# Maxima over hid's blocks from absolute values of the second butterfly stage, in place of one strided reduction

## The chip, the cores and the metric

One core of a Trainium2 chip runs the whole kernel. The metric is the device time of the program in microseconds, in the median of several runs. TensorE multiplies matrices into PSUM, VectorE and ScalarE work elementwise on SBUF and PSUM, GpSimd on SBUF alone, SyncE issues the transfers. The engines run their own instruction lists and wait for each other by semaphores.

## What is computed

The input x has 64 sequences of 64 tokens with 512 features. First x gets an attention layer's output added (a conditioned input, 16 heads, ALiBi); then a feed-forward layer's. The change lies in the second quantized product of that feed-forward layer:

```python
def fwht(x):                       # normalized Walsh-Hadamard transform of the last axis
    ...
def act_quant(x, bits):
    qb = float(2 ** (bits - 1) - 1)
    scale = qb / jnp.clip(jnp.max(jnp.abs(x), axis=-1, keepdims=True), EPS, None)
    q = jnp.clip(jnp.round(x * scale), -qb, qb) / scale
    return _ste(x, q)
def hbitlinear(x, w, bits):
    xq = act_quant(fwht(x), bits)
    wq = weight_quant(w)
    return jnp.einsum('bsd,fd->bsf', xq, wq)
h = hbitlinear(hidden_states, w_up, ACT_BITS)
h = jnp.square(jax.nn.relu(h))
return hbitlinear(h, w_down, ACT_BITS)      # 1024 features in, 512 out
```

Each token needs the largest absolute value over its 1024 transformed features.

## The kernel before

The 4096 tokens are cut into 32 pairs of sequences, 128 tokens each. The main loop has 35 steps, c = 0 to 34, and each engine has its own hand-written list for a step. Work on different pairs is staggered: in step c the attention of pair c runs, the output projection, residual and conditioning of pair c - 1, the feed-forward layer of pair c - 2 (which the code calls f), and the down product of pair c - 3. The conditioned input and the q and k products of later pairs (cond1, add_bias, copy_hi, split_lo, qk) fill up the steps while there are such pairs: add_bias until c = 27, qk until c = 29.

The 1024 hidden features of pair f lie as 8 blocks of 128 features by 128 tokens, features on partitions. Their transform has two parts: a 128x128 Hadamard product inside each block on TensorE (hadamard2), and three butterfly stages between the blocks on VectorE. fly0 reads PSUM and ScalarE's copy of the odd blocks and writes hid[:, 0]; fly1 goes from hid[:, 0] to hid[:, 1]; fly2 pairs block m with block m + 4 and goes from hid[:, 1] to hid[:, 0]. col_max then reduces hid[:, 0] over its 8 blocks to hid_max, 128 features by 128 tokens, largest absolute value. turn_max on TensorE transposes it to PSUM, max2 takes the largest of each token, and limit2, invert2, scale2 make the scale, which spread_scale on TensorE spreads over partitions. apply_scale2 multiplies hid[:, 0] by it and writes hid[:, 1]; round2 and clip2 follow, and down uses the result in the next step.

In the same part of a step, the first transform of pair c - 1 is under way: cond2 (TensorE), copy_g (ScalarE, gT), turn_g (GpSimd, two butterfly stages of two operations, gT to gT2 and back, each 128x256), hadamard1 (TensorE). For c = 32 those butterflies are VectorE's. The softmax of pair c is, too: exp (ScalarE), exp_sum and exp_recip (VectorE), normalize (GpSimd, two halves), turn_p (TensorE, two halves).

The order in a step around the change:

- TensorE: hadamard2(c-2), qk(c, 0), cond1(c+4), cond2(c-1), v_product(c), qk(c, 1), hadamard1(c-1), turn_max(c-2), turn_p(c, 0), qk(c, 2), turn_p(c, 1), spread_scale(c-2).
- VectorE: fly0, fly1, fly2 of c-2, add_bias(c+4), exp_sum(c, 1), col_max(c-2), exp_recip(c, 1), then the scale chains of c-1 (max1 to scale1) and c-2 (max2 to scale2) in turns.
- ScalarE: copy_odd(c-2), one copy of a qk product, exp(c, 1), copy_g(c-1), copy_v(c), further copies.
- GpSimd: turn_g(c-1), normalize(c, 0), normalize(c, 1), split_lo(c+4).

The buffer sq (8 blocks, the first half of late) holds the squared values of pair f from relu and square on; its last reader was square_lo, before fly0. The lines of the profile: L260 the butterflies on either engine, L904 col_max, L929 apply_scale2, L460 hadamard1, L493 turn_max, L418 turn_p, L354 every split product (q, k, v, o), L650 copy_g, L625 copy_v, L1063 normalize.

Of the kernel before, what the change touches and what calls it, by code (L numbers as in the profile page):

```python
# [21 lines left out]
ALU = mybir.AluOpType  # L22
ACT = mybir.ActivationFunctionType
AX = mybir.AxisListType
# [23 lines left out]
def adaln_attn_ffn(nc, x, idx1, bias_table, idx2, w1, wqT, wkT, wvT, woT, w2, upT, downT, cst, out):  # L48
    ctx = ExitStack()
    with ctx:  # L50
        def sb(name, shape, dt=F32):
            return ctx.enter_context(nc.sbuf_tensor(name, shape, dt))

        def sem(name):
            return ctx.enter_context(nc.semaphore(name))
# [46 lines left out]
        sq = late[:, 0:FF].rearrange("p (m t) -> p m t", m=FC)  # L102
        sq_hi = sb("sq_hi", [P, FC, P], F32R)
        sq_lo = sb("sq_lo", [P, FC, P], F32R)
        hid = sb("hid", [P, 2, FC, P])
        hid_odd = sb("hid_odd", [P, FC // 2, P])
        hid_max = sb("hid_max", [P, P])
# [51 lines left out]
        s_maxt = sem("s_maxt")  # L159
# [13 lines left out]
        a_sq = sem("a_sq")  # L173
        a_sqhi = sem("a_sqhi")
        a_odd = sem("a_odd")

        d_h = sem("d_h")
        d_hadr = sem("d_hadr")
# [14 lines left out]
        d_q1t = sem("d_q1t")  # L193
        d_sqlo = sem("d_sqlo")
        d_fly = sem("d_fly")
        d_colmax = sem("d_colmax")
        d_max2 = sem("d_max2")
        d_lim2 = sem("d_lim2")
# [21 lines left out]
        def pair(p):  # L220
            return 0 <= p < NPAIR
# [5 lines left out]
        def next_group(c):  # L227

            return 4 * c < LAST_JOB
# [4 lines left out]
        def cond_out(ps):  # L234

            return ps[:, :].rearrange("p (e n) -> p e n", e=2)[:, :, 0:KC * T].rearrange("p e (m t) -> p e m t", m=KC)
# [9 lines left out]
        def by_batch(t):  # L246
            return t.rearrange("p m (e t) -> p e m t", e=2)
# [346 lines left out]
        def _(act):  # L594
# [10 lines left out]
            def copy_hi(c):  # L605

                act.wait_ge(d_h, c + 1)
                act.activation(h_hi[:, (c // 2) % 2, :, (c % 2) * P:(c % 2) * P + P], h_sum[:, c % 2],
                               ACT.Copy).then_inc(a_hhi, 1)
# [6 lines left out]
            def copy_next_qk(c, n):  # L616
                job = 4 * c + n
                copy_qk(N_JOBS + job + 1, 1 + job // N_JOBS, job % N_JOBS, ring(c, (QK0, QK1, QK2, QK3)[n]))

            def copy_v(c):  # L620
                act.wait_ge(s_v, c + 1)
                blocks = ring(c, VAL).rearrange("t (a b n) -> t a b n", b=2, n=P)
                for e in range(2):
                    for b in range(2):
                        ins = act.activation(v_kd[b * T:b * T + T, c % 4, e], blocks[e * T:e * T + T, :, b, :], ACT.Copy)  # L625
                ins.then_inc(a_v, 1)

            def spread_k(c):
                act.wait_ge(a_qk, N_JOBS * (c // 2) + KC)
                t = slice((c % 2) * P, (c % 2) * P + P)  # L630
                for h in range(2):
                    ins = act.activation(k_bd[:, c % 2, :, h, :], kT[:, (c // 2) % 2, :, t], ACT.Copy, scale=slot_mask[:, h:h + 1])
                ins.then_inc(a_kbd, 1)

            def exp(c, half):
                hs = slice(8 * half, 8 * half + 8)
                act.wait_ge(d_less, 2 * c + half + 1)
                act.activation(s[:, c % 2, hs, :], s[:, c % 2, hs, :], ACT.Exp).then_inc(a_exp, 1)

            def copy_pt(c, r):  # L640
                act.wait_ge(s_pt, 2 * c + r + 1)
                act.activation(pT[:, r].rearrange("p a b -> p (a b)"), bank[r], ACT.Copy).then_inc(a_pt, 1)

            def copy_o(c):
                act.wait_ge(s_pv, c + 1)
                act.activation(by_bank(oT_hi[:]), pv_out, ACT.Copy).then_inc(a_ohi, 1)

            def copy_g(c):
                act.wait_ge(s_g, c + 1)
                act.activation(by_batch(gT[:]), cond_out(ps67), ACT.Copy).then_inc(a_g, 1)  # L650

            def scale_y1(f):
                act.wait_ge(d_scale1, f + 1)
                act.activation(y1[:, :], bank[6], ACT.Copy, bias=MAGIC, scale=sc1[:, f % 2, 3:4]).then_inc(a_y1, 1)

            def half_of(t, half):
                return t[:, 4 * half:4 * half + 4, :].rearrange("p a b -> p (a b)")

            def relu(f, half):
                act.wait_ge(s_up, 2 * f + half + 1)  # L660
                act.activation(half_of(sq, half), bank[4 + half], ACT.Relu).then_inc(a_relu, 1)  # L661

            def square(f, half):
                act.wait_ge(a_relu, 2 * f + half + 1)
                act.activation(half_of(sq, half), half_of(sq, half), ACT.Square).then_inc(a_sq, 1)

            def square_hi(f, half):
                act.wait_ge(a_sq, 2 * f + half + 1)
                act.activation(half_of(sq_hi, half), half_of(sq, half), ACT.Copy).then_inc(a_sqhi, 1)

            def copy_odd(f, half):
                act.wait_ge(s_f2, 2 * f + half + 1)
                odd = ps_f2[:, 4 * half:4 * half + 4].rearrange("p (a two) t -> p a two t", two=2)[:, :, 1]
                act.activation(hid_odd[:, 2 * half:2 * half + 2, :], odd, ACT.Copy).then_inc(a_odd, 1)  # L674

            def w_abs_sum(n, half):
                act.wait_ge(s_fraw[half], 16 * (n + 1))
                act.activation(ffn_half(n, half), ffn_stage(n, half), ACT.Abs, accum_out=wsum[:, n, half:half + 1]).then_inc(a_fsum, 1)

            def w_round(n, half):  # L680
                act.wait_ge(s_fsum, 3 * n + 3)
                st = ffn_stage(n, half)
                act.activation(st, st, ACT.Copy, bias=MAGIC, scale=wsum[:, n, 4:5]).then_inc(a_fround, 1)
# [27 lines left out]
            for c in range(N_STEP):  # L711
                if c == 2:

                    act.wait_ge(s_fclip, 4)
                if pair(c - 2):
                    relu(c - 2, 0)
                    square(c - 2, 0)
                    relu(c - 2, 1)
                    square_hi(c - 2, 0)
                    square(c - 2, 1)  # L720
                    square_hi(c - 2, 1)
                if pair(c):
                    exp(c, 0)
                if pair(c - 2):
                    copy_odd(c - 2, 0)
                    copy_odd(c - 2, 1)
                if next_group(c):
                    copy_next_qk(c, 0)
                if pair(c):
                    exp(c, 1)  # L730
                if c == 0:
                    w_round(0, 0)
                if c == 1:
                    w_abs_sum(1, 0)
                if pair(c - 1):
                    copy_g(c - 1)
                if c == 1:
                    w_abs_sum(1, 1)
                if pair(c):
                    if c == 0:  # L740
                        act.wait_ge(s_wlo, 4)
                    copy_v(c)
                if next_group(c):
                    copy_next_qk(c, 1)
                if c == 0:
                    w_round(0, 1)
                if pair(c + AHEAD):
                    copy_hi(c + AHEAD)
                if pair(c + 1):
                    spread_k(c + 1)  # L750
                if pair(c):
                    copy_pt(c, 0)
                if pair(c - 1):
                    scale_y1(c - 1)
                if next_group(c):
                    copy_next_qk(c, 2)
                if pair(c):
                    copy_pt(c, 1)
                if next_group(c):
                    copy_next_qk(c, 3)  # L760
                if pair(c):
                    copy_o(c)
                if c == 1:
                    w_round(1, 0)
                    w_round(1, 1)

        @block.vector
        def _(dve):
# [131 lines left out]
                butterflies(dve, hid[:, 1], hid[:, 0], 2, d_fly)  # L900

            def col_max(f):
                dve.wait_ge(d_fly, 8 * f + 8)
                dve.tensor_reduce(hid_max[:, :], hid[:, 0].rearrange("p m t -> p t m"), AX.X, ALU.max,  # L904
                                  apply_absolute_value=True).then_inc(d_colmax, 1)

            def max2(f):
                dve.wait_ge(s_maxt, f + 1)
# [17 lines left out]

            def apply_scale2(f):
                dve.wait_ge(s_scale, f + 1)
                dve.tensor_tensor(hid[:, 1], hid[:, 0], ps_scale.unsqueeze(1).broadcast_to([P, FC, P]), ALU.mult).then_inc(d_scaled, 1)  # L929

            def round2(f):
# [32 lines left out]
            for c in range(N_STEP):  # L964
# [44 lines left out]
                if pair(c - 2):  # L1009
                    col_max(c - 2)  # L1010
# [26 lines left out]
                if pair(c - 2):  # L1037
                    apply_scale2(c - 2)
# [110 lines left out]
```

## Time and profile before

| | us |
|---|---|
| median of 3 runs | 771.02 (769.98 to 771.21) |
| profiled execution, its own time | 770.51 |
| its span | 768.7 |
| TensorE busy | 724.3 (94%) |
| VectorE busy | 663.8 (86%) |
| ScalarE busy | 425.7 (55%) |
| GpSimd busy | 218.7 (28%) |

The span runs from the first instruction to the last; the device time is longer by what lies around it. Busy time is that in which an engine has an instruction under way. Matmul ends are modelled, and GpSimd's spans are rough. A row of the timeline has the start, the duration, the engine, the line, the operation, the result and its inputs with partitions x elements, a count, and in brackets the idle time ahead with what ended it. VectorE's and ScalarE's instructions overlap by some 0.1 us in the records: the next begins while the last result is written.

### The profile page before, as it was taken

The page shows a single profiled execution, that of the slowest core. Times are in us where ns is not written, and L with a number is a line of the kernel's source. Part 1 is how long each engine was busy: PE and PEld are TensorE (multiplying, and loading weights), DVE is VectorE, ACT ScalarE, POOL GpSimd, SP SyncE. Part 2 cuts the span into 40 slices and gives each one's busy share as a digit, 9 for nine tenths or more (in the row PEclk, how much of TensorE's full clock was granted, in tenths as well). Part 3 has the DMA queues.
Part 4 walks back from the last instruction along what each step waited for, and adds up shares of the span by engine and source line. Part 5 has one row for each costly group of instructions (what it writes and reads, how often), then busy time and mean ns, then how long its engine had stood idle before and what let it go on. Part 6 is the DMA issues. An engine that isn't in the chain of part 4 may idle for free.

```text
span 768.7 us, 23147 instructions
## 1 busy us (share of the span) xinstructions
PE 724.3 (94%) x9627; PEld 614.7 (80%) x9660; DVE 663.8 (86%) x1339; ACT 425.7 (55%) x847; POOL 218.7 (28%) x231
## 2 busy tenths in 40 slices
PE   6878699999999999999999999999999999998767
PEld 3867588888888888888888888888888888886543
DVE  3644899999999999999999999999999999899876
ACT  2656565655665565665565556565566556555421
POOL 1222123333332223333333222333333222223300
PEclk8989799999999999999999999999999999999999
DMA  8641011111101111111111111111110110010000
GB/s 281 223 134 36 1 36 50 50 49 50 49 23 44 36 50 49 50 49 50 49 33 36 47 37 50 49 50 50 50 48 23 59 31 24 23 29 18 15 14 27
DMA packets 37388, 39.90 MB, mean 52 GB/s; under 512 B 21156, under 2 KB 21284, under 8 KB 37284
## 3 DMA queue, kind: packets, MB, share of 16 engines
q1 hardware_dynamic: 34436, 33.48, 14.1%
q10 hardware_dynamic: 2848, 4.95, 1.8%
q8 instruction: 76, 1.25, 0.6%
q14 instruction: 28, 0.23, 0.1%
HBM read 30.02 MB, written 8.39 MB: 50 GB/s over the span
## 4 chain that ended last, share of the span: by engine, by line
PE 85%; DVE 5%; POOL 3%; issue 3%; ACT 2%; DMA 1%; SPq 1%; POOLq 0%; DVEq 0%
PE bank L354 44%; PE bank L478 8%; PE bank L514 7%; PE bank L460 4%; PE bank L378 4%; PE bank L344 4%; PE bank L487 4%; PE bank L418 3%; PE bank L435 3%; POOL gT L260 3%; PE bank L468 1%; PE bank L498 1%; DMA bias_in<-in_fside_8xS_dram 1%; DVE hid L260 1%; DVE hid L929 1%
## 5 line engine op out<-in xcount | busy, mean ns | idle before, releaser
L260 POOL TENSOR_TENSOR gT<-gT 128x256 f32<-128x256 f32 x124 | 107.9, 890 | 446.0 <-ACT gT L650 443.5
L260 DVE TENSOR_TENSOR hid<-hid 128x512 f32<-128x512 f32 x128 | 100.6, 827 | 0.0
L625 ACT ACTIVATE v_kd<-bank 64x256 f32<-64x256 f32 x128 | 48.5, 379 | 71.3 <-PE bank L354 70.2
L354 PE MATMUL bank<-h_hi,wk_hi 128*128 128x256 f32 x256 | 76.0, 297 | 3.2 <-POOL h_lo L1058 3.2
L354 PE MATMUL bank<-h_hi,wq_hi 128*128 128x256 f32 x256 | 74.3, 290 | 0.0
L478 PE MATMUL bank<-q1T,up_w 128*128 128x128 bf16 x1024 | 65.4, 224 | 9.2 <-DVE q1T L876 9.2
L354 PE MATMUL bank<-h_lo,wk_hi 128*128 128x256 f32 x256 | 73.1, 286 | 0.0
L354 PE MATMUL bank<-h_hi,wk_lo 128*128 128x256 f32 x256 | 73.0, 285 | 0.0
L661 ACT ACTIVATE late<-bank 128x512 f32<-128x512 f32 x64 | 37.6, 588 | 62.5 <-PE bank L478 62.5
L478 PEld LDWEIGHTS bank<-q1T,up_w 128*128 128x128 bf16 x1024 | 59.7, 100 | 14.8 <-DVE q1T L876 9.8
L354 PE MATMUL bank<-h_hi,wq_lo 128*128 128x256 f32 x256 | 71.5, 279 | 0.0
L354 PE MATMUL bank<-h_lo,wq_hi 128*128 128x256 f32 x256 | 71.5, 279 | 0.0
L1063 POOL TENSOR_TENSOR s<-s,srow 128x512 f32<-128x512 f32 x64 | 67.6, 1058 | 13.1 <-issue 6.9
L904 DVE TENSOR_REDUCE hid_max<-hid 128x128 f32<-128x1024 f32 x32 | 63.0, 1970 | 0.1
L674 ACT ACTIVATE hid_odd<-bank 128x256 f32<-128x256 f32 x64 | 24.6, 384 | 62.2 <-PE bank L487 59.6
L929 DVE TENSOR_TENSOR hid<-hid,bank 128x1024 f32<-128x1024 f32 x32 | 39.1, 1221 | 22.3 <-PE bank L498 22.3
L354 PE MATMUL bank<-wo_hi,oT_hi 128*128 128x512 f32 x128 | 56.6, 442 | 0.4 <-DVE oT_lo L836 0.4
L514 PE MATMUL bank<-down_w,q2T 128*128 128x512 bf16 x225 | 54.3, 382 | 2.1 <-DVE q2T L937 0.3
L354 PE MATMUL bank<-wv_hi,h_hi 128*128 128x512 f32 x128 | 54.5, 426 | 0.0
L354 PEld LDWEIGHTS bank<-h_hi,wk_hi 128*128 128x128 f32 x256 | 49.9, 195 | 5.0 <-POOL h_lo L1058 3.4
L354 PE MATMUL bank<-wv_hi,h_lo 128*128 128x512 f32 x128 | 51.2, 400 | 0.0
L354 PE MATMUL bank<-wv_lo,h_hi 128*128 128x512 f32 x128 | 51.2, 400 | 0.0
(117 smaller groups left out, 1933.1 us busy)
## 6 DMA issues: line engine op xcount, KB each, us to landing
x_in<-in_x_dram SPq DMA_DIRECT2D x32, 256.0 KB, 2.7
x_res<-in_x_dram SPq DMA_DIRECT2D x32, 256.0 KB, 3.3
out_dram<-late SPq DMA_DIRECT2D x32, 256.0 KB, 3.4
w_in<-in_L_cond_weights_dram SPq DMA_DIRECT2D x126, 16.0 KB, 2.3
bias_in<-in_fside_8xS_dram SPq DMA_DIRECT2D x62, 32.0 KB, 2.9
k_bd<-in_L_attn_Wk_dram ACTq DMA_DIRECT2D x1, 1024.0 KB, 5.6
s<-in_L_attn_Wq_dram ACTq DMA_DIRECT2D x1, 1024.0 KB, 8.5
v_kd<-in_L_attn_Wv_dram ACTq DMA_DIRECT2D x1, 1024.0 KB, 10.7
```

Of the source, the lines that this page charges most:

```text
L260: eng.tensor_tensor(dv[:, :, n], sv[:, :, 0], sv[:, :, 1], op).then_inc(done, 1)
L344: mm = pe.matmul(dst[f * T:f * T + T, e, m, :], tokens[r, n:n + T], w[r, :], start=True, stop=True)
L354: mm = pe.matmul(dst, lhs(a, k), rhs(b, k), start=(k == 0 and n == 0), stop=(k == KC - 1 and n == 2))
L378: mm = pe.matmul(dst[:, m // 2, m % 2], qT[rows, (c // 2) % 2, m, t0:t0 + T], k_bd[rows, c % 2, m, :, e * T:e * T + T], start=True, stop=True)
L460: mm = pe.matmul(bank[6][:, m * P:(m + 1) * P], gT[:, m, :], had, start=True, stop=True)
L478: mm = pe.matmul(ps45[:, m * P:(m + 1) * P], up_w[:, k, m * P:(m + 1) * P], q1T[:, k, :], start=(k == 0), stop=(k == KC - 1))
L514: mm = pe.matmul(ring(f + 3, DOWN), q2T[:, k, :], down_w[:, k, :], start=(k == 0), stop=(k == FC - 1))
L625: ins = act.activation(v_kd[b * T:b * T + T, c % 4, e], blocks[e * T:e * T + T, :, b, :], ACT.Copy)
L661: act.activation(half_of(sq, half), bank[4 + half], ACT.Relu).then_inc(a_relu, 1)
L904: dve.tensor_reduce(hid_max[:, :], hid[:, 0].rearrange("p m t -> p t m"), AX.X, ALU.max, apply_absolute_value=True).then_inc(d_colmax, 1)
L929: dve.tensor_tensor(hid[:, 1], hid[:, 0], ps_scale.unsqueeze(1).broadcast_to([P, FC, P]), ALU.mult).then_inc(d_scaled, 1)
L1063: pool.tensor_tensor(s[:, c % 2, hs, :], s[:, c % 2, hs, :], srow[:, 2, hs].unsqueeze(2).broadcast_to([P, 8, T]), ALU.mult).then_inc(p_pn, 1)
```

## The change

For two blocks a and b, the larger of |a + b| and |a - b| is |a| + |b|. So the largest absolute value over fly2's outputs is the largest, over m = 0 to 3, of |hid1[m]| + |hid1[m + 4]|, with hid1 what fly1 left in hid[:, 1]. ScalarE now takes the absolute value of hid[:, 1] into sq (absolute, 128x1024), behind copy_g. VectorE's col_max becomes three operations that depend on each other: one addition (128x512) and a maximum (128x256), both in place in sq, and a maximum (128x128) into hid_max. fly2 stays as it was. New semaphores a_abs and d_abs order this; relu waits until the maxima of the pair before have been taken from sq, and apply_scale2, which overwrites hid[:, 1], waits for absolute.

```diff
+        a_abs = sem("a_abs")
...
+        d_abs = sem("d_abs")
...
             def relu(f, half):
                 act.wait_ge(s_up, 2 * f + half + 1)
+                if half == 0 and f >= 1:
+
+                    act.wait_ge(d_colmax, f)
                 act.activation(half_of(sq, half), bank[4 + half], ACT.Relu).then_inc(a_relu, 1)
...
+            def absolute(f):
+                act.wait_ge(d_fly, 8 * f + 6)
+                act.wait_ge(d_sqlo, 2 * f + 2)
+                act.activation(sq, hid[:, 1], ACT.Abs).then_inc(a_abs, 1)
...
                 if pair(c - 1):
                     copy_g(c - 1)
+                if pair(c - 2):
+                    absolute(c - 2)
...
             def col_max(f):
-                dve.wait_ge(d_fly, 8 * f + 8)
-                dve.tensor_reduce(hid_max[:, :], hid[:, 0].rearrange("p m t -> p t m"), AX.X, ALU.max,
-                                  apply_absolute_value=True).then_inc(d_colmax, 1)
+
+                dve.wait_ge(a_abs, f + 1)
+                dve.tensor_tensor(sq[:, 0:4, :], sq[:, 0:4, :], sq[:, 4:8, :], ALU.add).then_inc(d_abs, 1)
+                dve.wait_ge(d_abs, 2 * f + 1)
+                dve.tensor_tensor(sq[:, 0:2, :], sq[:, 0:2, :], sq[:, 2:4, :], ALU.max).then_inc(d_abs, 1)
+                dve.wait_ge(d_abs, 2 * f + 2)
+                if f >= 1:
+                    dve.wait_ge(s_maxt, f)
+                dve.tensor_tensor(hid_max[:, :], sq[:, 0, :], sq[:, 1, :], ALU.max).then_inc(d_colmax, 1)
...
             def apply_scale2(f):
                 dve.wait_ge(s_scale, f + 1)
+                dve.wait_ge(a_abs, f + 1)
                 dve.tensor_tensor(hid[:, 1], hid[:, 0], ps_scale.unsqueeze(1).broadcast_to([P, FC, P]), ALU.mult).then_inc(d_scaled, 1)
```

VectorE's list in a middle step before, from fly2 (L260) over add_bias (L784), exp_sum (L827), col_max (L904) and exp_recip (L832) to max1 (L848):

```order
L260 TENSOR_TENSOR hid<-hid 128x512 x2
L784 TENSOR_TENSOR h_sum<-bank,bias_in 128x2x4x64
L827 TENSOR_REDUCE srow<-s 128x8
L904 TENSOR_REDUCE hid_max<-hid 128x128
L832 RECIPROCAL srow<-srow 128x8
L848 TENSOR_REDUCE sc<-bank 128x1
```

The same place with the change, where the line numbers are shifted (L262 is fly2, L917 to L923 the new col_max, late the buffer of sq):

```order
L262 TENSOR_TENSOR hid<-hid 128x512 x2
L796 TENSOR_TENSOR h_sum<-bank,bias_in 128x2x4x64
L839 TENSOR_REDUCE srow<-s 128x8
L917 TENSOR_TENSOR late<-late 128x512
L919 TENSOR_TENSOR late<-late 128x256
L923 TENSOR_TENSOR hid_max<-late 128x128
L844 RECIPROCAL srow<-srow 128x8
L860 TENSOR_REDUCE sc<-bank 128x1
```

One instruction has become three, in the same place; nothing else moves on VectorE.

ScalarE's list with the change, from exp (L640) and copy_g (L652) over absolute (L684) to copy_v (L627) and copy_hi (L610):

```order
L640 ACTIVATE s<-s 128x512
L652 ACTIVATE gT<-bank 128x2x4x64
L684 ACTIVATE late<-hid 128x1024
L627 ACTIVATE v_kd<-bank 64x256 x4
L616 ACTIVATE kT<-bank 128x256
L610 ACTIVATE h_hi<-h_sum 128x4x128
```

L684 is new between the copy of gT and the four copies of v; the rest of ScalarE's list, and the lists of TensorE, GpSimd and SyncE, are those of before.

## Rows read from the trace of the kernel before

**Rows 1.** The page's part 4: shares of the span on the chain, by engine.

```profile
PE 85%; DVE 5%; POOL 3%; issue 3%; ACT 2%; DMA 1%; SPq 1%; POOLq 0%; DVEq 0%
```

**Rows 2.** Windows, one middle step: stretch, busy us of each engine, granted clock.

```profile
core 0: us, PE busy (x) PEld busy (x) DVE busy (x) ACT busy (x) POOL busy (x), PEclk, DMA share, GB/s
432.40:453.90 21.50, 21.45 (x300) 18.63 (x300) 19.94 (x42) 12.62 (x26) 6.69 (x7) 1.00 0.15 46
```

**Rows 3.** Waits of TensorE: for whom, us in total, times, longest.

```profile
PE bank L460 <- POOL gT L260: 6.5, 5, 2.6
PE bank L493 <- DVE hid_max L904: 5.1, 3, 3.2
```

**Rows 4.** Timeline, TensorE, c = 18, around hadamard1, turn_max and turn_p.

```profile
441.26 0.28 PE L354 MATMUL bank<-h_hi,wk_lo 128*128 128x256 f32 x1
441.42 1.16 PE L460 MATMUL bank<-cst_sb,gT 128*128 128x128 f32 x8
442.41 0.31 PE L493 MATMUL bank<-cst_sb,hid_max 128*128 128x128 f32 x1
442.56 0.27 PE L418 MATMUL bank<-cst_sb,s 128*128 128x128 f32 x1
```

**Rows 5.** Timeline, GpSimd (POOL), c = 18: the four butterfly operations, normalize.

```profile
437.89 0.80 POOL L260 TENSOR_TENSOR gT<-gT 128x256 f32<-128x256 f32 x1 [14.56 <-ACT gT L650]
438.65 1.19 POOL L260 TENSOR_TENSOR gT<-gT 128x256 f32<-128x256 f32 x1
439.92 0.74 POOL L260 TENSOR_TENSOR gT<-gT 128x256 f32<-128x256 f32 x1
440.62 0.74 POOL L260 TENSOR_TENSOR gT<-gT 128x256 f32<-128x256 f32 x1
441.33 1.03 POOL L1063 TENSOR_TENSOR s<-s,srow 128x512 f32<-128x512 f32 x1
```

**Rows 6.** Timeline, VectorE (DVE), c = 18: fly2, add_bias, col_max, max2.

```profile
437.41 0.68 DVE L260 TENSOR_TENSOR hid<-hid 128x512 f32<-128x512 f32 x1
438.01 1.23 DVE L260 TENSOR_TENSOR hid<-hid 128x512 f32<-128x512 f32 x1
439.16 0.68 DVE L784 TENSOR_TENSOR h_sum<-bank,bias_in 128x512 f32<-128x512 f32 x1
...
440.36 1.98 DVE L904 TENSOR_REDUCE hid_max<-hid 128x128 f32<-128x1024 f32 x1
...
443.22 0.28 DVE L909 TENSOR_REDUCE sc<-bank 128x1 f32<-128x128 f32 x1
```

**Rows 7.** Line L904, 107 to 640 us: duration ns min/median/max, first and last start.

```profile
L904 DVE TENSOR_REDUCE hid_max<-hid x25: 1978/1981/1983, 118.2 to 633.8; 128x128 f32<-128x1024 f32 x25
```

**Rows 8.** The page's part 5: busy us, mean ns | idle us before.

```profile
L661 ACT ACTIVATE late<-bank 128x512 f32<-128x512 f32 x64 | 37.6, 588 | 62.5 <-PE bank L478 62.5
```

**Rows 9.** Timeline, ScalarE (ACT), c = 18: copy_g, copy_v.

```profile
437.21 0.60 ACT L650 ACTIVATE gT<-bank 128x512 f32<-128x512 f32 x1 [0.22 <-PE bank L344]
440.17 1.16 ACT L625 ACTIVATE v_kd<-bank 64x256 f32<-64x256 f32 x3 [2.36 <-PE bank L354]
```

**Rows 10.** Timeline, c = 28: col_max, GpSimd's third butterfly operation, hadamard1.

```profile
654.69 2.00 DVE L904 TENSOR_REDUCE hid_max<-hid 128x128 f32<-128x1024 f32 x1
...
654.85 0.74 POOL L260 TENSOR_TENSOR gT<-gT 128x256 f32<-128x256 f32 x1
...
656.34 1.16 PE L460 MATMUL bank<-cst_sb,gT 128*128 128x128 f32 x8 [0.33 <-POOL gT L260]
```

**Rows 11.** Timeline and windows, c = 30: hadamard1; PEclk third from the end.

```profile
698.63 2.07 PE L460 MATMUL bank<-cst_sb,gT 128*128 128x128 f32 x8 [2.56 <-POOL gT L260]
698.60:700.70 2.10, 2.07 (x9) 2.00 (x10) 1.93 (x2) 0.41 (x1) 1.07 (x2) 0.50 0.00 0
```

**Rows 12.** Timeline, VectorE, c = 33: col_max.

```profile
757.07 1.88 DVE L904 TENSOR_REDUCE hid_max<-hid 128x128 f32<-128x1024 f32 x1
```

## The prediction, made before the changed kernel ran

> **What bounds the kernel now.** I read the shares of the chain that ended last first, then the busy time of a middle stretch, then instruction by instruction the place where the chain is closest to another engine. The chain is TensorE for 85% [rows 1], and one middle step of 21.5 us has 21.45 us of TensorE and 19.94 us of VectorE at full granted clock [rows 2]. The whole list of TensorE's waits has two entries that touch this change: hadamard1 on GpSimd's gT (6.5 us in 5 waits) and turn_max on hid_max (5.1 us in 3 waits, all in the last three steps) [rows 3]. So in the middle, VectorE's share of 93% costs nothing by itself, and making it less busy gains nothing there.
>
> But these two edges are met with nothing to spare. In the step that I follow (c = 18), the last product before hadamard1 starts at 441.26 and hadamard1 at 441.42 [rows 4], a gap of 0.16 us where such products follow each other by some 0.12 us. GpSimd's fourth butterfly operation ends at 440.62 + 0.74 = 441.36 [rows 5]: hadamard1 starts as soon as gT is there. The column maxima end at 440.36 + 1.98 = 442.34 [rows 6], and turn_max starts at 442.41 [rows 4]. The first turn_p starts at 442.56, GpSimd's normalize(c, 0) ended at 441.33 + 1.03 = 442.36. A delay of gT moves TensorE one for one, a delay of hid_max by all but the 0.07 us, one of normalize by all but 0.2 us. The column maxima have the same length in every middle step (1.978 to 1.983 us, 25 of them, to 633.8 us) [rows 7], and with the first one there are 26 such steps, c = 2 to 27.
>
> **How VectorE and GpSimd get in each other's way.** fly2 is two additions of the same form as the new one: both inputs in SBUF, 128x512 f32. The first one has 0.68 us and the next starts 0.60 us later. The second starts at 438.01 and VectorE goes on only at 439.16 [rows 6]: 1.15 us instead of 0.60. GpSimd's first butterfly was running (437.89, 0.80), and its second, begun at 438.65, took 1.19 us where the third and fourth take 0.74 [rows 5]. This reads as taking turns: VectorE stood until 439.16 - 0.60 = 438.56 (0.67 us after GpSimd's start), then GpSimd stood until 439.16 and needed 0.68 us more. The reduction that is now removed ran beside GpSimd's third and fourth butterfly and normalize(c, 0), and they keep 0.74, 0.74 and 1.03 us: an operation with one SBUF input does not hold GpSimd up. That is what the change gives away. The Trainium skill (SBUF — State Buffer, engine ports) says that the pair of ports shared by VectorE and GpSimd is an exclusive lock held for a whole instruction, taken by a VectorE operation with two SBUF inputs against a GpSimd one that reads SBUF, and never by tensor_reduce. The trace agrees in both halves; without the lock the sum would be the first rival's.
>
> **The change, part by part, at c = 18.** *ScalarE, absolute:* 128x1024. A 128x512 takes 588 ns [rows 8]; 512 more elements can't cost more than a second such instruction, so 0.6 to 1.2 us; I take 1.0, as start and end are paid once. It can start when copy_g (437.21, 0.60) is issued and fly1 is done (the second fly1 operation is over before 437.41 + 0.1), so about 437.8, and ends at 438.8, by 439.0 at the high end. copy_v starts at 440.17 after 2.36 us of idle time [rows 9]: the idle time holds it, cost nothing; without that cover it would delay v_kd and with it pv by up to 1.2 us. VectorE wants the result at 440.36, so its wait ends at once. The waits on a_abs in apply_scale2 and on d_colmax in relu are met steps earlier. No DMA, nothing on SP's queue, and no instruction of TensorE or GpSimd moves.
>
> *VectorE, three operations alone:* 128x512 is 0.68 us [rows 6]. 128x128 elements take 0.28 us (the small maximum at 443.22) [rows 6], so 128x256, between them on a line, is 0.41. Each depends on the one before, with 0.02 us for the semaphore. Alone: 0.68 + 0.41 + 0.28 + 0.04 = 1.41 us, against 1.88 us of the reduction alone [rows 12]. The first also need not wait for the end of fly2, another 0.1 us.
>
> *Together with GpSimd:* (1) the addition is ready at 440.36, GpSimd's third butterfly (439.92) holds until 440.59, so the addition runs 440.59 to 441.19. (2) GpSimd's fourth starts its work at 441.19 and ends 0.68 later, 441.87 in place of 441.36. hadamard1 moves by **0.51 us**. (3) The first maximum, ready at 441.30, waits for that butterfly until 441.80 and ends its turn at 442.13. (4) normalize(c, 0), issued about 441.84, waits until then, holds for 1.0 us and ends at 443.1. (5) The last maximum needs the first one's result at 442.24 and finds GpSimd in normalize: it runs from 443.1 and is written at 443.36. turn_max would be due at 442.41 + 0.51 = 442.92 and starts at 443.40: **0.48 us** more. (6) The first turn_p follows at 443.55 in place of 442.56: normalize is done by then. Together 1.0 us a step. Queued behind the last maximum on VectorE are exp_recip(c, 1) and the scale chain; they move by the same 1.0 us, the second normalize too, and TensorE, a microsecond late itself, finds them ready. Bounds for a step: 0.51 (only the first delay) to 1.25 (second rival). 26 steps by 1.0: +26.0 us.
>
> *c = 28 and 29:* no add_bias, so VectorE is ready at 654.69, ahead of the third butterfly (654.85) [rows 10]. The addition goes first (to 655.29), butterfly to 655.97, maximum to 656.23, fourth butterfly to 656.91, where it ended about 656.28 (hadamard1 starts at 656.34 after waiting 0.33 us). 0.65 a step, turn_max not late any more: +1.3 us. *c = 30 and 31:* gT is late already (hadamard1 at 698.63) [rows 11] and done before VectorE gets to the addition; only the second half of the price is left, 0.5 each: +1.0 us. *c = 32 and 33:* no butterflies and no normalize on GpSimd; the reduction (1.88 us at 757.07 [rows 12], and its like in c = 32) is on the chain in full. Each gives 1.88 - 1.41 + 0.1 = 0.57: -1.1 us.
>
> Sum: 26.0 + 1.3 + 1.0 - 1.1 = +27.2 us. The profiled execution took 770.5 us (span 768.7 and 1.8 around it), so 797.7 us; the median of the runs is 0.5 us higher, inside what can be told (0.2% or 1.5 us).
>
> **The rivals.**
> *No turns taken here (other side).* fly2's lengthening might come from something else, its blocks in hid for instance, and the new operations on late might pass GpSimd freely. Then only the tail's -1.1 us is left: 769.4 us, faster, or nothing that can be told if a little is given back. For it: GpSimd's records are rough. Against: both engines' starts fit the turns to 0.02 us. It decides if GpSimd's fourth butterfly is held less than 0.04 us a step (1.1 / 26). The Trainium skill (VectorE: DVE Perf Modes, rules for kernel authors) calls tensor_reduce on a hot path the slowest operation and advises restructuring; the trace agrees on its length. By that rule the sum would be this rival's. Chance 0.09.
> *GpSimd's fourth butterfly gets in ahead of the addition.* Release at 440.59 and its issue at 440.62 are 0.03 us apart. gT is then on time; the addition runs to 441.9, normalize to 442.9, first maximum to 443.2, the last, ready at 443.3, is written at 443.6: turn_max 1.25 us late. 26 x 1.25 + 1.2 = +33.7, 804.2 us. Chance 0.12.
> *Only the first delay.* The maxima slip between GpSimd's operations, or start a little sooner than I think: 26 x 0.51 + 1.2 = +14.5, 785.0 us. For it: the last maximum is short. Against: its input is ready just as normalize is waiting. Chance 0.14.
> *The clock falls too.* After 2.56 us without work at c = 30, hadamard1 runs 2.07 us at a granted clock of 0.50 (1.2 GHz), against 1.16 at full clock [rows 10, 11]. If stalls of 0.5 us did this everywhere: 26 x 0.91 more, 821 us. Against: 0.33 us of waiting at c = 28 did not. Chance 0.05.
> That the change doesn't do what it says (absolute late, VectorE waiting for it) would need ScalarE to be 1.4 us later than worked out; it is inside the spread of the others.
>
> **How the numbers follow.** Forecast 0.60. Its own uncertainty is 0.1 us a step, 2.6 us in all. The range takes in the third rival's 785.0 and the second's 804.2 with this margin: 782 to 807 us; it leaves out the first and the last, 0.14 together, and a little of the rest. Slower by over 0.2% are all but the first rival: 0.91; faster 0.07, within 0.2% 0.02, which share the first rival.
>
> **What would show it.** Steps of 22.5 us in place of 21.5, still with granted clock 1.00; a fourth butterfly of 1.2 us, so gT's group longer by 0.5 us in its four; TensorE waits some 0.5 us on gT and 0.5 us on hid_max in 26 steps, where there were none; the addition some 0.9 us, the last maximum 0.9 to 1.1 us in the records; normalize(c, 0) 0.3 us longer; no wait of VectorE on absolute; VectorE's maxima done in 1.4 us in c = 32 and 33. I am wrong if the step keeps its 21.5 us, or if TensorE waits for something other than these two.

## The result, and the profile after

The changed kernel takes 795.99 us in the median of 6 executions (791.05 to 798.47), the kernel before 770.38 us. The ratio is 1.0327, with a 95% interval of 1.0286 to 1.0369: slower by 3.3%, inside the predicted range. The execution that was profiled is the shortest: 791.05 us, span 788.9 us, mean granted clock 0.981. Of the ten executions of this kernel, here and in the first experiment below, two have a clock of 0.976 or more and take 791 us, eight have 0.966 to 0.972 and take 795.3 to 798.5 us; where that difference lies is shown there.

The first view is the page's shares of the chain that ended last, for the changed kernel, by engine and by line:

```profile
span 788.9 us, 23369 instructions
...
PE 56%; DVE 31%; issue 5%; ACT 4%; POOL 3%; DMA 1%; SPq 1%; POOLq 0%; DVEq 0%
PE bank L356 24%; DVE hid L262 9%; PE bank L480 8%; PE bank L516 7%; DVE hid L904 5%; PE bank L380 4%; PE bank L420 4%; DVE hid_max L923 3%; PE bank L437 3%; DVE late L919 3%; DVE late L917 3%; DVE srow L839 2%; DVE h_sum L796 2%; PE bank L489 2%; POOL gT L262 2%
```

TensorE's share fell from 85% [rows 1] to 56%, and VectorE's rose from 5% to 31%: in a middle step the chain now leaves TensorE for VectorE's butterflies and the new operations. TensorE's waits between 107 and 640 us (for whom, us in total, times, longest), where the kernel before has none at all:

```profile
PE bank L462 <- POOL gT L262: 7.6, 24, 0.3
PE bank L495 <- DVE hid_max L923: 4.2, 24, 0.2
```

The two waits are 0.32 and 0.17 us a step, 0.49 together, less than what the step grows by. A wait counts only from the modelled end of the product before, and before the change hadamard1 started 0.12 us ahead of that end [rows 4] and turn_max 0.17: the starts moved by 0.44 and 0.34 us.

One middle step in the timeline of the changed kernel, by engine: GpSimd (L262 the third and fourth butterfly operation, L1082 normalize), VectorE (L917 addition, L919 and L923 maxima), ScalarE (L684 absolute, L627 copy_v), TensorE (L462 hadamard1, L495 turn_max).

```profile
453.04 0.74 POOL L262 TENSOR_TENSOR gT<-gT 128x256 f32<-128x256 f32 x1
453.74 1.18 POOL L262 TENSOR_TENSOR gT<-gT 128x256 f32<-128x256 f32 x1
454.88 1.23 POOL L1082 TENSOR_TENSOR s<-s,srow 128x512 f32<-128x512 f32 x1
...
453.48 0.85 DVE L917 TENSOR_TENSOR late<-late 128x512 f32<-128x512 f32 x1
454.36 0.84 DVE L919 TENSOR_TENSOR late<-late 128x256 f32<-128x256 f32 x1
455.24 1.02 DVE L923 TENSOR_TENSOR hid_max<-late 128x128 f32<-128x128 f32 x1
...
450.82 1.05 ACT L684 ACTIVATE late<-hid 128x1024 f32<-128x1024 f32 x1
453.28 1.55 ACT L627 ACTIVATE v_kd<-bank 64x256 f32<-64x256 f32 x4 [1.41 <-PE bank L356]
...
454.98 1.16 PE L462 MATMUL bank<-cst_sb,gT 128*128 128x128 f32 x8 [0.32 <-POOL gT L262]
456.31 0.33 PE L495 MATMUL bank<-cst_sb,hid_max 128*128 128x128 f32 x1 [0.17 <-DVE hid_max L923]
```

The fourth butterfly, begun at 453.74, takes 1.18 us where it took 0.74 [rows 5]; normalize 1.23 for 1.03. The addition takes 0.85 us and the two maxima 0.84 and 1.02. In the tail, with GpSimd idle, the same three take 0.68, 0.42 and 0.29 us. From the addition's start to hid_max it is 2.78 us, against 1.98 of the one reduction [rows 6]. The step from one hadamard1 to the next is 22.32 us in the mean of 26 (97.85 at c = 2 to 678.10 at c = 28), against 21.48 us before (97.75 to 656.34).

The two spans differ by 20.2 us: +0.1 until c = 2, +21.7 from there to c = 28, +0.6 to c = 30, +0.5 to c = 32, and -2.6 from the last hadamard1 to the end. In that last piece the granted clock differs too (1.00 after, 0.95 before), so not all of the 2.6 us is the shorter maxima; from c = 30 to c = 32 it is 0.91 after and 0.96 before.

### The profile page after: what moved, and what is told of

It is laid out like the page before. It is cut to its first block, busy times and chain, and to the rows that moved or that the text cites. A ratio compares the mean times of both kernels' runs of the same rounds, so it can differ in the third digit from the quotient of the medians.

```text
span 788.9 us, 23369 instructions
## 1 busy us (share of the span) xinstructions
PE 731.7 (93%) x9627; PEld 614.4 (78%) x9660; DVE 679.2 (86%) x1403; ACT 467.3 (59%) x879; POOL 236.5 (30%) x231
## 3 DMA queue, kind: packets, MB, share of 16 engines
q8 instruction: 76, 1.25, 0.7%
## 4 chain that ended last, share of the span: by engine, by line
PE 56%; DVE 31%; issue 5%; ACT 4%; POOL 3%; DMA 1%; SPq 1%; POOLq 0%; DVEq 0%
PE bank L356 24%; DVE hid L262 9%; PE bank L480 8%; PE bank L516 7%; DVE hid L904 5%; PE bank L380 4%; PE bank L420 4%; DVE hid_max L923 3%; PE bank L437 3%; DVE late L919 3%; DVE late L917 3%; DVE srow L839 2%; DVE h_sum L796 2%; PE bank L489 2%; POOL gT L262 2%
## 5 line engine op out<-in xcount | busy, mean ns | idle before, releaser
L262 POOL TENSOR_TENSOR gT<-gT 128x256 f32<-128x256 f32 x124 | 120.5, 992 | 445.6 <-ACT gT L652 443.2
L262 DVE TENSOR_TENSOR hid<-hid 128x512 f32<-128x512 f32 x128 | 100.8, 829 | 0.0
L1082 POOL TENSOR_TENSOR s<-s,srow 128x512 f32<-128x512 f32 x64 | 73.5, 1152 | 18.0 <-DVE srow L844 10.4
L627 ACT ACTIVATE v_kd<-bank 64x256 f32<-64x256 f32 x128 | 48.4, 378 | 41.0 <-PE bank L356 39.9
L462 PE MATMUL bank<-cst_sb,gT 128*128 128x128 f32 x256 | 38.6, 296 | 16.1 <-POOL gT L262 16.1
```

The lines of the kernel that those rows point to most:

```text
L262: eng.tensor_tensor(dv[:, :, n], sv[:, :, 0], sv[:, :, 1], op).then_inc(done, 1)
L462: mm = pe.matmul(bank[6][:, m * P:(m + 1) * P], gT[:, m, :], had, start=True, stop=True)
L1082: pool.tensor_tensor(s[:, c % 2, hs, :], s[:, c % 2, hs, :], srow[:, 2, hs].unsqueeze(2).broadcast_to([P, 8, T]), ALU.mult).then_inc(p_pn, 1)
```

## The experiments

All times are medians beside the kernel before on the same chip. "Step" is the mean distance from one hadamard1 to the next in the profiled execution of that kernel, between c = 2 and c = 27.

| run | VectorE's two-input operations in col_max | step, us | ratio to before, 95% |
|---|---|---|---|
| before | none | 21.48 | |
| the change | all three in SBUF | 22.32 | 1.0327 (1.0286 to 1.0369) |
| the change again | all three in SBUF | 22.33 | 1.0357 (1.0333 to 1.0381) |
| absolute alone | none | 21.49 | 1.0033 (1.0012 to 1.0054) |
| addition, then reduction | addition in SBUF | 21.91 | 1.0192 (1.0161 to 1.0222) |
| the same, addition from PSUM | none with both in SBUF | 21.47 | 0.9986 (0.9965 to 1.0008) |
| addition from PSUM, maxima in SBUF | maxima in SBUF | 21.84 | 1.0117 (1.0094 to 1.0141) |
| all from PSUM | none with both in SBUF | 21.47 | 0.9976 (0.9962 to 0.9990) |
| only in c = 32 and 33 | none in the middle | 21.49 | 0.9975 (0.9951 to 0.9998) |
| fly2 from PSUM, and the tail | fly2 freed as well | 21.30 | 0.9936 (0.9917 to 0.9954) |

### The change again

The same kernel as the change, unedited, to see what spreads its times.

> The changed kernel once more, to see what spreads its times over 791 to 798 us. Theory (turns between VectorE's two-SBUF-input operations and GpSimd): the middle step is 22.3 us again, and a slower execution differs only by which engine gets its turn first in a race of 0.03 us, so its middle steps are longer (up to 22.7 us, 1.25 us a step over before) at granted clock 1.00. Rival: the middle steps are the same 22.3 us in each execution and the spread comes from the granted clock at the head or the tail, so an execution of 796 us shows a lower clock there, of about 0.966 in the mean.

796.88 us (795.29 to 798.45). Its profiled execution has a span of 794.5 us, 5.6 us more than the first. Windows of both in the tail (stretch, busy us of each engine, then the granted clock, third from the end); first the change as profiled at first, then this run:

```profile
740.00:760.00 20.00, 16.35 (x191) 12.28 (x194) 15.66 (x37) 8.54 (x18) 4.46 (x4) 0.91 0.04 14
```

```profile
740.00:760.00 20.00, 15.47 (x154) 11.91 (x156) 13.32 (x30) 8.62 (x17) 5.61 (x5) 0.74 0.04 14
```

The 26 middle steps take 580.2 and 580.5 us, both at granted clock 1.00. From c = 30 to c = 32 it is 38.5 us in the first and 43.4 us in this one, where the clock is 0.74 in place of 0.91; TensorE there waits for other engines (four waits, 4.5 us of the 20), and its busy time is lower than in the middle. The rival holds in these two executions: their difference lies in the tail, with its lower clock, and not in the turns. For the other eight only the mean clock is on record. Among the 19 executions of the kernel before beside these runs the same is seen in smaller measure: 14 at 0.976 or more take 767.7 to 772.5 us, five at 0.969 to 0.973 take 772.0 to 775.0 us. Eight of the change's ten executions are at 0.972 or less, and three of these 19: the lower clock looks more frequent with the change. Why was not tested. It bears on the price: of the 25.6 us between the first two medians, the two profiled executions show 20.5; the other 5 fit the lower clock in the tail.

### Absolute alone

```diff
             def col_max(f):
-                dve.wait_ge(a_abs, f + 1)
-                dve.tensor_tensor(sq[:, 0:4, :], sq[:, 0:4, :], sq[:, 4:8, :], ALU.add).then_inc(d_abs, 1)
...
-                dve.tensor_tensor(hid_max[:, :], sq[:, 0, :], sq[:, 1, :], ALU.max).then_inc(d_colmax, 1)
+                dve.wait_ge(d_fly, 8 * f + 8)
+                dve.tensor_reduce(hid_max[:, :], hid[:, 0].rearrange("p m t -> p t m"), AX.X, ALU.max,
+                                  apply_absolute_value=True).then_inc(d_colmax, 1)
```

> ScalarE's absolute values stay, with all waits, but VectorE takes the maxima with the one strided reduction of before; the absolute values are not used. Theory (turns on VectorE's two-input operations): the time of before, 770 us (ratio 1.00), step 21.5 us. Rival (ScalarE's added instruction delays copy_v, or its reading of hid beside fly2 costs something): most of the 25 us stay, 790 us or more.

773.11 us, ratio 1.0033. The step is 21.49 us, 0.01 more than before, TensorE has no wait between 107 and 640 us, and the four butterflies have their 869 ns in the mean. ScalarE's 1.05 us a step and its reading of hid beside fly2 cost the middle nothing. The interval lies just above 1. The profiled execution (span 769.1) has a granted clock of 0.85 in its last 34 us, where before it has 0.95, and six of the ten executions are at 0.972 or less, against three of the 19 before. That the 0.3% is the tail's clock fits this but isn't shown.

### The addition, then a short reduction

```diff
                 dve.tensor_tensor(sq[:, 0:4, :], sq[:, 0:4, :], sq[:, 4:8, :], ALU.add).then_inc(d_abs, 1)
-                dve.wait_ge(d_abs, 2 * f + 1)
-                dve.tensor_tensor(sq[:, 0:2, :], sq[:, 0:2, :], sq[:, 2:4, :], ALU.max).then_inc(d_abs, 1)
-                dve.wait_ge(d_abs, 2 * f + 2)
+                dve.wait_ge(d_abs, f + 1)
...
-                dve.tensor_tensor(hid_max[:, :], sq[:, 0, :], sq[:, 1, :], ALU.max).then_inc(d_colmax, 1)
+                dve.tensor_reduce(hid_max[:, :], sq[:, 0:4, :].rearrange("p m t -> p t m"), AX.X, ALU.max).then_inc(d_colmax, 1)
```

> Only the addition of the change, with both inputs in SBUF, then one strided reduction over the four sums in place of the two maxima. Theory: the addition delays GpSimd's fourth butterfly by 0.45 us, and the reduction of half the length (about 1.05 us) lets GpSimd go on, so hid_max is early and only hadamard1 waits: step 21.5 + 0.45 = 21.95 us, in all 770.4 + 26 x 0.45 + 2 = about 784 us (780 to 787). Rival (the cost is in the chain of dependent operations on VectorE, not in the turns): this chain takes 0.69 + 1.05 = 1.76 us, shorter than the 1.98 of before, so 769 to 771 us.

783.56 us, where the theory had about 784. A middle step of this kernel, GpSimd's four butterflies, VectorE's two operations and TensorE:

```profile
445.33 3.92 POOL L262 TENSOR_TENSOR gT<-gT 128x256 f32<-128x256 f32 x4 [14.74 <-ACT gT L652]
...
447.81 0.85 DVE L917 TENSOR_TENSOR late<-late 128x512 f32<-128x512 f32 x1
448.70 1.06 DVE L921 TENSOR_REDUCE hid_max<-late 128x128 f32<-128x512 f32 x1
...
449.31 1.16 PE L462 MATMUL bank<-cst_sb,gT 128*128 128x128 f32 x8 [0.32 <-POOL gT L262]
450.30 0.27 PE L495 MATMUL bank<-cst_sb,hid_max 128*128 128x128 f32 x1
```

The butterflies take 3.92 us (3.47 before), hadamard1 waits 0.32 us, and turn_max follows 0.99 us later as it did before, with no wait on hid_max: the chain of two is over at 449.76, well before it is wanted. VectorE's own work has become shorter (0.85 + 1.06 against 1.98 us), and the kernel is still 1.9% slower. The step is 0.43 us longer.

### The same addition, with one input in PSUM

Against the run above:

```diff
-                act.activation(sq, hid[:, 1], ACT.Abs).then_inc(a_abs, 1)
+                act.activation(sq[:, 0:4, :], hid[:, 1, 0:4], ACT.Abs)
+                act.activation(ps_f2[:, 0:4], hid[:, 1, 4:8], ACT.Abs).then_inc(a_abs, 1)
...
-                dve.tensor_tensor(sq[:, 0:4, :], sq[:, 0:4, :], sq[:, 4:8, :], ALU.add).then_inc(d_abs, 1)
+                dve.tensor_tensor(sq[:, 0:4, :], ps_f2[:, 0:4], sq[:, 0:4, :], ALU.add).then_inc(d_abs, 1)
```

> As the run with the addition and a short reduction, but ScalarE writes half of the absolute values (four blocks) to a PSUM bank that is free then, in two instructions of 128x512, so that the addition has one input in PSUM and one in SBUF. Theory (turns only with two SBUF inputs): GpSimd's four butterflies take 3.47 us again, no new wait of TensorE, step 21.5 us, 769 to 770.5 us. Rival (any VectorE operation with two inputs holds GpSimd up, or ScalarE's work costs): as the run with both inputs in SBUF, about 784 us.

769.42 us, ratio 0.9986: no difference from before that can be told, and 14 us less than the run above, from which it differs only in where one input of one VectorE operation lies, and in ScalarE writing that half with a second instruction. Groups between 107 and 640 us of this kernel (busy us, mean ns), GpSimd's butterflies and the addition:

```profile
L262 POOL TENSOR_TENSOR gT<-gT 128x256 f32<-128x256 f32 x100 | 85.0, 871 | 370.3 <-ACT gT L652 368.4
...
L917 DVE TENSOR_TENSOR late<-bank,late 128x512 f32<-128x512 f32 x25 | 16.9, 675 | 0.0
```

871 ns is the mean of the kernel before (870), and the addition takes its 0.68 us. In the run with both inputs in SBUF the same groups have 981 and 848 ns. This pair shows the cause of the first half: two inputs in SBUF, beside a GpSimd operation.

### The maxima in SBUF, the addition not

The edit is that of the run above, with the change's two maxima, both inputs in SBUF, kept behind the addition.

> The addition has one input in PSUM (as in the run with the addition from PSUM), but the two maxima after it are those of the change, with both inputs in SBUF. Theory: the addition leaves GpSimd's fourth butterfly alone, so hadamard1 is on time; the first maximum waits for that butterfly and runs to about 0.3 us behind it, normalize(c, 0) then holds the last maximum up: hid_max is 0.5 us late. Step 21.5 + 0.5 = 22.0 us, TensorE waits on hid_max alone, in all about 784 us (780 to 787). Rival (the addition is what costs, and the maxima only follow it): 770 us.

780.94 us beside 772.26 of before: near the theory's lower end, far from the rival's. One middle step:

```profile
442.31 3.48 POOL L262 TENSOR_TENSOR gT<-gT 128x256 f32<-128x256 f32 x4 [14.54 <-ACT gT L652]
445.75 1.22 POOL L1083 TENSOR_TENSOR s<-s,srow 128x512 f32<-128x512 f32 x1
...
444.79 0.67 DVE L918 TENSOR_TENSOR late<-bank,late 128x512 f32<-128x512 f32 x1
445.50 0.57 DVE L920 TENSOR_TENSOR late<-late 128x256 f32<-128x256 f32 x1
446.10 1.02 DVE L924 TENSOR_TENSOR hid_max<-late 128x128 f32<-128x128 f32 x1
...
445.84 1.16 PE L462 MATMUL bank<-cst_sb,gT 128*128 128x128 f32 x8
447.17 0.33 PE L495 MATMUL bank<-cst_sb,hid_max 128*128 128x128 f32 x1 [0.17 <-DVE hid_max L924]
```

GpSimd's butterflies have their 3.48 us, and hadamard1 is on time. The last maximum of 128 elements takes 1.02 us behind normalize, turn_max starts 1.33 us behind hadamard1 in place of 0.99, and the step is 0.36 us longer. So the two halves are 0.43 (addition) and 0.36 us (maxima), 0.79 together; the change has 0.84.

### All from PSUM

ScalarE's two instructions are those of the run with the addition from PSUM; col_max becomes:

```diff
             def col_max(f):
...
+                dve.tensor_tensor(sq[:, 0:2, :], ps_f2[:, 0:2], sq[:, 0:2, :], ALU.add).then_inc(d_abs, 1)
+                dve.tensor_tensor(ps_f2[:, 2:4], ps_f2[:, 2:4], sq[:, 2:4, :], ALU.add).then_inc(d_abs, 1)
+                dve.wait_ge(d_abs, 4 * f + 2)
+                dve.tensor_tensor(sq[:, 0, :], ps_f2[:, 2], sq[:, 0, :], ALU.max).then_inc(d_abs, 1)
+                dve.tensor_tensor(ps_f2[:, 3], ps_f2[:, 3], sq[:, 1, :], ALU.max).then_inc(d_abs, 1)
+                dve.wait_ge(d_abs, 4 * f + 4)
...
+                dve.tensor_tensor(hid_max[:, :], ps_f2[:, 3], sq[:, 0, :], ALU.max).then_inc(d_colmax, 1)
```

> The change's arithmetic with no VectorE operation that has two SBUF inputs: ScalarE writes half of the absolute values to PSUM, and addition and maxima are cut into five operations, each with one input in PSUM. Theory: step 21.47 us, four butterflies 3.47 us, the maxima done in about 1.6 us in each step and the tail as short as the change's: 769 us (0.998 of before). Rival (a chain of dependent operations costs, the more the longer; this one has three waits in place of two): at least the 25 us of the change, 796 us or more.

770.26 us beside 772.26 of before, ratio 0.9976. Five operations in a chain of three levels, in a middle step:

```profile
440.91 0.41 DVE L917 TENSOR_TENSOR late<-bank,late 128x256 f32<-128x256 f32 x1
...
442.22 0.29 DVE L925 TENSOR_TENSOR hid_max<-bank,late 128x128 f32<-128x128 f32 x1
```

hid_max is there 1.60 us after the first one's start, in place of 1.98 by the reduction, and the step stays 21.47 us: the middle gains nothing from a shorter VectorE, as the prediction had it. In the tail, turn_max's two waits for hid_max fall from 3.15 and 1.26 us to 2.78 and 0.69, 0.9 us together; the rest of the 2.0 us between the medians is not placed.

### Only in the tail

```diff
+NEW = NPAIR - 2
...
             def col_max(f):
+                if f < NEW:
+                    dve.wait_ge(d_fly, 8 * f + 8)
+                    dve.tensor_reduce(hid_max[:, :], hid[:, 0].rearrange("p m t -> p t m"), AX.X, ALU.max,
+                                      apply_absolute_value=True).then_inc(d_colmax, 1)
+                    return
...
```

ScalarE's absolute, too, is issued for f >= NEW only, and the semaphore counts are adapted.

> The change in c = 32 and 33 alone, where GpSimd has nothing to do; the strided reduction in all steps before. Theory: step 21.48 us, and the two reductions of 1.88 us on the chain become 1.3 us: 0.57 us a step, 1.1 us in all, 769 us (ratio 0.9985). Rival (a tail that is not bound by these maxima): 770.4 us, ratio 1.000; no execution may show the 22.3 us of the change.

770.55 us, ratio 0.9975, its interval from 0.9951 to 0.9998 just below 1. In c = 33 of this kernel:

```profile
757.97 0.68 DVE L923 TENSOR_TENSOR late<-late 128x512 f32<-128x512 f32 x1
758.69 0.42 DVE L925 TENSOR_TENSOR late<-late 128x256 f32<-128x256 f32 x1
759.15 0.29 DVE L928 TENSOR_TENSOR hid_max<-late 128x128 f32<-128x128 f32 x1
```

The three are done in 1.47 us where the reduction took 1.88 [rows 12]; with the 0.1 us that the first no longer waits for fly2, 0.5 us in each of two steps. In these two steps, with GpSimd idle, the operations are a gain of 1.0 us. The medians differ by 1.7 us, more than that explains, and the interval nearly reaches 1: the whole time agrees with the gain but doesn't measure it.

### fly2 from PSUM, and the tail

```diff
             def fly1(f):
...
+                for n, op in enumerate((ALU.add, ALU.subtract)):
+                    dve.tensor_tensor(hid[:, 1, 2 * n:2 * n + 2], hid[:, 0, 0:2], hid[:, 0, 2:4], op).then_inc(d_fly, 1)
+                    dve.tensor_tensor(ps_f2[:, 2 * n:2 * n + 2], hid[:, 0, 4:6], hid[:, 0, 6:8], op).then_inc(d_fly, 1)
...
             def fly2(f):
...
+                for n, op in enumerate((ALU.add, ALU.subtract)):
+                    dve.tensor_tensor(hid[:, 0, 4 * n:4 * n + 4], hid[:, 1, 0:4], ps_f2[:, 0:4], op).then_inc(d_fly, 1)
```

This is for c up to 31; c = 32 and 33 are those of the run above.

> The change only in c = 32 and 33, and until c = 31 fly1 writes the upper four blocks to a free PSUM bank (four operations of 128x256), so that fly2's two operations have one input in SBUF and pass GpSimd's butterflies. Theory: the four butterflies fall from 3.47 to 2.95 us; TensorE had nothing to wait for in the middle, so the step stays 21.45 us, hadamard1 at c = 28 and 29 no longer waits (0.33 us each), at c = 30 and 31 it comes 0.5 to 0.9 us sooner; with the tail's 1.1 us in all 3 us, 767.5 us (ratio 0.996). Rival (fly2's long second operation and the long second butterfly have another cause than their inputs): butterflies 3.47 us as before and 769 us.

766.76 us beside 772.26, ratio 0.9936: faster than both kernels, and 0.7 us below what I expected. Groups of this kernel between 107 and 640 us, the butterflies and fly2:

```profile
L263 POOL TENSOR_TENSOR gT<-gT 128x256 f32<-128x256 f32 x100 | 71.8, 739 | 370.5 <-ACT gT L656 368.5
...
L926 DVE TENSOR_TENSOR hid<-hid,bank 128x512 f32<-128x512 f32 x50 | 32.2, 684 | 0.0
```

All four butterflies now take 739 ns (870 before), fly2's operations 684 ns: the turns in fly2 [rows 5, 6] were the inputs' doing as well. The expectation missed on the step, which it had at 21.45 us: it is 21.30, and the steps into c = 28 and 29 are 20.83 us where they were 21.48 and 21.45. From c = 2 to c = 30 this kernel gains 7 us; 4.5 of them are gone again from c = 30 to c = 32, at a clock of 0.84 in place of 0.96. In the kernel before, then, TensorE did lose 0.18 us a step. Its weight loads show where, first in the kernel before, then in this one:

```profile
441.15 0.19 PEld L354 LDWEIGHTS bank<-h_hi,wk_lo 128*128 128x128 f32 x1
441.41 0.30 PEld L460 LDWEIGHTS bank<-cst_sb,gT 128*128 128x128 f32 x2
```

```profile
436.41 0.19 PEld L360 LDWEIGHTS bank<-h_hi,wk_lo 128*128 128x128 f32 x1
436.53 0.19 PEld L466 LDWEIGHTS bank<-cst_sb,gT 128*128 128x128 f32 x1
```

Such loads follow each other by 0.12 us, as this one does here; in the kernel before it came after 0.26: gT was 0.14 us late in each step, too little to be listed as a wait. turn_max's load gains another 0.08 us (0.90 us behind hadamard1's in place of 0.98), of which the loads for turn_p give back some 0.05.

## Why the prediction was right, point by point

- **The bound before, and what has no slack.** Right, and understated. Nothing shorter on VectorE moved the middle (21.47 us in the run with all from PSUM), and delays of gT and hid_max went straight to TensorE. I called hadamard1 just on time; it was 0.14 us late by the weight loads, and removing that, with 0.08 us at turn_max, was worth 0.18 us a step in the last experiment.
- **The turns.** Right. The addition went first and the fourth butterfly stood, and the last maximum stood behind normalize: 1.02 us in place of 0.29, more than the doubling that two operations sharing a port evenly would give. The Trainium skill's rule (SBUF — State Buffer, Who interferes with whom) of an exclusive hold for two SBUF inputs agrees with this and with the pair of runs that differ in one input's place, 783.56 and 769.42 us. That reductions pass freely agrees as well: the short one took 1.06 us beside GpSimd's operations and 1.02 with GpSimd idle. Of the signs that I named, the waits came out smaller (0.32 and 0.17 us, not 0.5 and 0.5, because the records overlap), and normalize(c, 0) was 0.2 us longer, not 0.3.
- **ScalarE's absolute, 1.0 us, at no cost.** Right: 1.05 us, and copy_v's idle time fell from 2.36 to 1.41 us. Absolute alone left the step at 21.49 us.
- **The three operations alone, 0.68, 0.41, 0.28.** Measured 0.68, 0.42, 0.29. From one record's end to the next one's start it is 0.04 us, where I had 0.02: 1.47 us in all, not 1.41.
- **The two halves, 0.51 + 0.48 us.** Both somewhat too large: the fourth butterfly took 1.18 us, not 1.25 (3.92 us for the four, +0.45), and turn_max came 1.33 us behind hadamard1 in place of 0.99 (+0.34). Each hold ended some 0.1 us sooner than I had read from the records; why, no run shows. 0.84 a step in place of 1.0: +21.7 us in 26 steps where I had 26.0. This is the term that was most mis-sized.
- **c = 28 to 31.** Forecast 2.3 us, measured 1.1 us in the first profile (0.6 and 0.5). The mechanism at c = 28 was as forecast: the addition went first, turn_max was not late, and hadamard1 waited 0.88 us where it had waited 0.33, so 0.55 more, not 0.65. By my count of pieces, which runs from hadamard1 to hadamard1, c = 28's share stands among the 26 steps. The second piece holds effects of the clock.
- **The tail, -1.1 us.** The operations bear it out (0.5 us in each of two steps). The first profile's tail is 2.6 us shorter, but its clock is other than before's.
- **The sum** was 797.7 us against 795.99. Made against its own execution, 770.5 us with 20.5 us measured on it, it was 6.7 us too high: 4.3 in the middle, 1.2 at c = 28 to 31, 1.5 in the tail, less 0.4 at the start and outside the span. The median lies nearer because most executions of the change have a lower clock, in the one that was profiled in the tail: a term that I did not have. That the two errors nearly cancel is luck.
- **The rivals.** No turns: excluded by the fourth butterfly's 1.18 us in place of 0.74. GpSimd ahead of the addition: not seen in either profile; the addition was served first and the fourth butterfly waited. Only the first delay: excluded, turn_max waits too. The clock in the middle: stayed 1.00. In the tail it moved by 5 us between two executions.

## What to carry to other kernels

A VectorE operation with two SBUF inputs was not free beside GpSimd's operations, though VectorE had time to spare: look what GpSimd is doing at that moment and who waits for it. The slower reduction with one input (1.98 us a step, against 1.47 for the three alone) was the better neighbour; giving the two-input operation one input in PSUM took the conflict away (butterflies of 871 ns in the mean, not 981). Before replacing an operation on a busy engine, find the steps in which it is on the chain (here two of 32) and change it only there.

## What the runs showed of the hardware

- An operation of 128 elements a partition (0.29 us alone) took 1.02 us in every middle step, since it came up while GpSimd held normalize.
- The same program's middle came out equal to 0.3 us in 580 us in two executions, and its tail differed by 5 us from c = 30 to c = 32, with granted clocks of 0.91 and 0.74 in 740 to 760 us. TensorE was busy for 16.35 and 15.47 us of these 20; what decides between the two was not found.
- A late input cost 0.14 us a step without standing in the waits: the spacing of weight loads showed it (0.26 us in place of 0.12).
